# Graph message stage: a tile's two counts as one two-column product, with the right-hand columns copied into a small ring by ScalarE

## The reference, cut to what matters

```
es, ev = ys[dst], yv[dst]
m0a = wA * es * sh0
m0b = wD * einsum('eud,ed->eu', ev, sh1) * INV_SQRT3
m1a = wB[:, :, None] * es[:, :, None] * sh1[:, None, :]
m1b = wC[:, :, None] * ev * sh0[:, :, None]
ns  = segment_sum(concatenate([m0a, m0b], axis=1), src, num_segments=N)
nv  = segment_sum(concatenate([m1a, m1b], axis=1), src, num_segments=N)
deg = segment_sum(ones(n_edges), src, num_segments=N)
os_ = (ns * dn[:, None]) @ w2_s * inv2 + sc_s        # dn = rsqrt(max(deg, 1))
```

## Time and profile before

| | |
|---|---|
| time, median of 3 runs | 6061.02 us (6052.65 to 6061.88) |
| the profiled execution, its own time | 6073.1 us |
| its span, first to last instruction | 6071.4 us |
| PE busy | 5657.3 us, 93% |
| PEld busy | 4550.0 us, 75% |
| DVE busy | 5431.3 us, 89% |
| ACT busy | 3457.0 us, 57% |
| POOL busy | 4647.0 us, 77% |
| stage (c), first to last scatter start | 2655.0 to 5760.7 us |

### The profile page before, as it was taken

How to read it: one execution, slowest core, us unless ns; L and a number is a source line. 1 busy time by engine, 2 the same in 40 slices (tenths; PEclk the granted TensorE clock), 3 DMA queues, 4 the chain that set the end, 5 groups by cost and what they waited for, 6 DMA issues and landing times.

```text
span 6071.4 us, 211848 instructions
## 1 busy us (share of the span) xinstructions
PE 5657.3 (93%) x41086; PEld 4550.0 (75%) x41087; DVE 5431.3 (89%) x17528; ACT 3457.0 (57%) x12685; POOL 4647.0 (77%) x3868
## 2 busy tenths in 40 slices
PE   7899999999999997789999999999999999999876
PEld 5455555555555555579999999999999999999765
DVE  2899999999999998989999999999999999999777
ACT  2566666666666665655555555555555555555466
POOL 2777777777777774458888888888888888888877
PEclk9899999999999999999999999999999999999999
DMA  6799999999999996469999999999999999999997
GB/s 202 216 269 267 268 269 267 266 268 267 266 267 267 266 268 182 136 148 178 178 178 178 178 177 177 178 175 176 178 176 177 178 177 176 176 177 175 155 278 229
DMA packets 1269411, 1272.43 MB, mean 210 GB/s; under 512 B 220911, under 2 KB 1205744, under 8 KB 1269264
## 3 DMA queue, kind: packets, MB, share of 16 engines
q0 software_dynamic: 328176, 468.28, 46.2%
q1 hardware_dynamic: 941186, 803.62, 45.7%
HBM read 682.35 MB, written 588.89 MB: 209 GB/s over the span
## 4 chain that ended last, share of the span: by engine, by line
PE 52%; DMA 14%; issue 11%; DVE 9%; SPq 4%; DVEq 4%; ACT 3%; POOL 2%; ACTq 0%; POOLq 0%
DMA part<-arena,c_idx 13%; PE PS L905 10%; PE PS L1008 9%; PE PS L990 8%; PE PS L895 6%; PE PS L979 6%; PE PS L1023 6%; PE PS L1006 4%; SPq L437 2%; DVE big L1279 2%; DVEq L362 2%; POOL part L603 2%; DVE big L1217 1%; PE PS L846 1%; DVE big L1225 1%
## 5 line engine op out<-in xcount | busy, mean ns | idle before, releaser
L603 POOL DMA_INDIRECT part<-arena,c_idx x1664 | 2596.6, 1560 | 530.2 <-issue 341.5
L574 POOL DMA_INDIRECT big<-h_tab,big x1664 | 1631.6, 981 | 526.0 <-issue 364.4
L905 PE MATMUL PS<-big 128*128 128x260 f32 x3328 | 972.5, 411 | 155.6 <-DVE big L1217 148.6
L1008 PE MATMUL PS<-w2m,arena 128*128 128x128 f32 x6656 | 1103.7, 288 | 0.0
L905 PEld LDWEIGHTS PS<-big 128*128 128x128 f32 x3328 | 556.1, 189 | 443.4 <-issue 333.1
L1008 PEld LDWEIGHTS PS<-w2m,arena 128*128 128x128 f32 x6656 | 876.9, 192 | 0.0
L990 PE MATMUL PS<-arena 128*128 128x256 f32 x3328 | 860.7, 381 | 15.3 <-ACT arena L781 14.8
L1225 DVE TENSOR_TENSOR big<-big,PS 128x260 f32 x1664 | 700.0, 421 | 168.7 <-PE PS L905 118.5
L678 ACT ACTIVATE big<-PS,arena 128x128 f32<-128x128 f32 x1664 | 513.3, 359 | 502.7 <-PE PS L895 501.4
L780 ACT COPY arena<-PS 128x512 f32<-128x512 f32 x832 | 488.8, 588 | 545.0 <-DMA part<-arena,c_idx 493.3
L757 ACT COPY arena<-PS 128x384 f32<-128x384 f32 x1664 | 719.2, 487 | 28.4 <-PE PS L979 3.0
(11 more groups left out here) (194 smaller groups left out, 10950.0 us busy)
## 6 DMA issues: line engine op xcount, KB each, us to landing
w_tab<-big SPq DMA_DIRECT2D x416, 520.0 KB
arena<-w_tab SPq DMA_DIRECT2D x1664, 130.0 KB
part<-arena SPq DMA_DIRECT2D x1664, 32.1 KB
ot_tab<-big SPq DMA_DIRECT2D x416, 128.0 KB
arena<-ot_tab SPq DMA_DIRECT2D x416, 128.0 KB
arena<-src_tab SPq DMA_DIRECT2D x416, 128.0 KB
big<-part SPq DMA_DIRECT2D x392, 128.5 KB, 3.0
big<-h_tab,big POOLq DMA_INDIRECT x1664
```

The costliest lines, as they stand in the source:

```text
L574: pool.indirect_dma_start(hg[:, s, k, :], None, h_tab, bass.IndirectOffsetOnAxis(ap=sidx[:, s, k:k + 1], axis=0)).then_inc(s_hg[s], 16)
L603: pool.indirect_dma_start(part[q], bass.IndirectOffsetOnAxis(ap=c_idx[:, s, k:k + 1], axis=0), o_cmb[:, s, k, :], None, compute_op=ALU.add ...
L905: mm(PS[:, 2 + k % 2, 0:HW], oh[:, p, k, :], hg[:, p, k, :], start=True, stop=True).then_inc(s_agg, 1)
L1008: last = mm(o_v[:, k, 2 * j:2 * j + 2, :].rearrange("p j u -> p (j u)"), midT[:, k, 1 + j, :], w2m[:, (1 + 2 * j) * MUL:(3 + 2 * j) * MUL] ...
```

## The change

Three edits. TensorE's `count` now makes one product of two columns for each tile in place of two products of one column, so its weights are loaded once for a tile and not twice. Its right-hand side is `c_vr`, a new ring of four slots with two tiles of two bf16 columns each. The second column of all of it (`rank`) is written once by VectorE at the start of the program, in place of the copy to `rank_b`. The first (`valid`) is written by ScalarE in each step, just ahead of its copy to `c_sh`. Two waits come with it: ScalarE waits for `s_ccnt` before it overwrites a slot, and TensorE's `count` waits for `s_csh`, the semaphore of the copy to `c_sh`.

```diff
-        rank_b = sb("rank_b", [P, 1], BF16)
...
+        c_vr = sb("c_vr", [P, TURN, PAIR, 2], BF16)
...
                 if there(u):
                     wait(act, s_cw[s], landed(u, s, PAIR))
                     wait(act, s_cov, u - 3)
+                    wait(act, s_ccnt, u - 3)
+                    a.copy(c_vr[:, s, :, 0], valid[:, ds(u * PAIR, PAIR)])
                     a.copy(c_sh[:, s, :, :], wt[:, s, :, D + 1:D + 4]).then_inc(s_csh, 1)
...
                 def count():
                     wait(pe, s_cnum, u - 3)
+                    wait(pe, s_csh, u - 2)
                     for k in range(PAIR):
-                        eq = same[:, o, k, :].bitcast(BF16)[:, 1::2]
-                        mm(counts[:, k, 0:1], eq, valid[:, ds((u - 3) * PAIR + k, 1)], start=True, stop=True)
-                        last = mm(counts[:, k, 1:2], eq, rank_b[:, :], start=True, stop=True)
+                        last = mm(counts[:, k, :], same[:, o, k, :].bitcast(BF16)[:, 1::2], c_vr[:, o, k, :],
+                                  start=True, stop=True)
                     last.then_inc(s_ccnt, 1)
...
-            v.tensor_copy(rank_b[:, :], rank)
+            v.tensor_copy(c_vr[:, :, :, 1], rank_i[:, 0:1].bitcast(F32).to_broadcast([P, TURN * PAIR]).rearrange(
+                "p (s k) -> p s k", s=TURN))
```

## The result

The change makes the kernel slower: 6101.58 us (median of 4 runs, 6096.34 to 6105.8) against 6060.51, a ratio of 1.0065 (95% interval 1.0052 to 1.0078). In a later group of five rounds on one chip it was 1.0056 (1.0042 to 1.007). The forecast was 6058, in a range of 6036 to 6080.

What follows compares the result with a forecast made beforehand. GpSimd's scatter pitch, 3.695 us a step, was taken to bound stage (c). Of 5.0 us waiting for data 3 came off, the 28.3 us of longer scatters stayed: 6061.0 - 3 = 6058 us, range 6036 to 6080.

Steps and rivals of the forecast that it cites:

- GpSimd's pitch bounds the stage: Stage (c): GpSimd's scatters, 3.695 us a step, set the pace; at most 33.3 of TensorE's 41.6 us can be had.
- bare pitch: GpSimd in stage (c): 1663 start-to-start distances of 1.8475 us, unstretched and without waits, 3072.4 us.
- TensorE's pitch 3.65 us, ScalarE's copy and the waits at no cost: Stage (c): TensorE's step falls from 3.70 to 3.65 us; ScalarE's 0.2 us copy is hidden, the new waits cost nothing.
- Where TensorE's time goes: Stage (c): ScalarE's 493 us wait on landed scatters rises by about 40, TensorE's on ScalarE from 14.8 to 30-50.
- the 28.3: Stage (c): 28.3 us by which some scatters run longer than the median, left unchanged in the forecast.
- The DMA variant: DMA engines have no room, so landings get later with any gain, ending at the forecast; chance 0.61 together with it.
- The slower rival: Stage (c): VectorE's L1388 moves over scatter starts and holds them up to 0.2 us; at most 33 us more; chance 0.17.
- at the edge: Stage (c): VectorE's comparison in a quiet stretch runs 0.07 us over the next scatter's start without lengthening it.
- the sign set for this rival, 1575: Profile after: a mean scatter (L603) above 1575 ns would show that other VectorE operations came over scatter starts.
- The scatter is held until about its end: GpSimd: a two-SBUF-input VectorE operation still running some 0.1 us after a scatter's start holds the scatter until it finishes.

Runs made afterwards that it cites:

- f3: Kernel before, four count products kept, with c_src loaded ahead of wt and VectorE's comparison moved ahead in its step; ratio 0.9963 to the kernel before.
- f4: Kernel before with only the load of c_src moved ahead of the loads of wt; ratio 0.9947 to the kernel before.
- g2: The same kernel as f4, run on another chip; ratio 0.9969 to the kernel before there.
- e1: Kernel before plus ScalarE's new copy and both new waits, counts still made in four products; ratio 1.0004 to the kernel before.
- e2: Changed kernel with each two-column product made twice, so TensorE's pitch is back at 3.70 us; ratio 1.0000 to the kernel before.
- e6: Changed kernel with the load of c_src moved ahead of the two loads of wt; ratio 0.9990 to the kernel before.
- e8: Changed kernel with VectorE's 128x512 comparison cut into two of 128x256; ratio 1.0033 to the kernel before.
- g1: The same kernel as e6, run again on the chip of g2; ratio 0.9996 to the kernel before.
- f1: Changed kernel unaltered, measured again in a later group; ratio 1.0056 to the kernel before.

## Why the prediction was wrong

- *GpSimd's pitch bounds the stage*: right. The bare pitch held in every run, and the best of them stand 7 to 12 us above 3072.4. TensorE ended early as before (21.0 us idle ahead of stage (d)), and its saving bought nothing. Only in f3, f4 and g2, which keep the four products and have hardly a scatter held, is TensorE at 3.700 us the slower of the two, by 0.005 us a step.
- *TensorE's pitch 3.65 us, ScalarE's copy and the waits at no cost*: right, within 0.14% (e1, e2).
- *Where TensorE's time goes*: its wait on ScalarE rose to 61.1 us, above the 30 to 50 forecast; ScalarE's wait on landed scatters rose by 182 us, not by 40.
- *"A late landing throws VectorE back over a scatter's start just as before, since that phase is set by the landing and not by TensorE. So I leave the 28.3."* This is the step that failed. The phase is set by the landing, but the landing is set by SyncE's loads, and these follow TensorE and VectorE. They go out 0.2 us earlier against the scatter in the median, `c_src` before 1.7 us in 106 cases instead of 14, and the scatter then lands 0.5 to 1 us later. ScalarE's copy, TensorE and VectorE are thrown back, and the comparison lies over the next scatter's start. The term measured 56.6 us instead of 28.3, and with e2, e6 and e8, which each weaken one link, 26, 37 and 18 us of the scatters' time come back.
- *The DMA variant*: I wrote that later landings end "at the forecast too". They don't: GpSimd had no more to wait for (6.7 us left, against 5.0), but behind the late landings more scatters were held.
- *The slower rival* named the right place, a VectorE operation over a scatter's start, and gave at most 33 us more. The operation was wrong: L1388 made 0.9 us, and the comparison that was already at the edge made 47.7 of the 56.6. The mean of 1577 ns passed the sign set for this rival, 1575.
- *"The scatter is held until about its end"*, for an operation that runs on some 0.1 us after the start: borne out. Up to 0.12 us of overlap the comparison held none; beyond that the hold grew with the overlap, less 0.12 us.

What stays open: why a load issued 1.5 us after the scatter's start goes with a later landing than one issued at 0.1 or 2.3 us, and whether it is `c_src` or the pair of `wt` ahead of it. The trace shows when, not how the packets queue. And why stage (a) is slower on the second chip, where it moved 203 GB/s (g1, 400 to 2300 us) against 268 (f1), stays open too.

## What to carry to other kernels

Before you speed up an engine, take the pitch of each engine from start to start; where a second one has the same pitch, the saving can't come out, and the quicker engine runs up against the ring between them. Then ask what the quicker engine will issue earlier, and beside which transfer that lands: here the kernel lost 0.6% by 0.05 us a step of TensorE, and the kernel before gained 0.5% by moving one 128 KB load ahead of two others. Here a producer a little slower than its consumer (3.700 against 3.695 us) kept the ring empty and the late transfers harmless.

## What the runs showed of the hardware

- At the same traffic an indirect scatter's landing differs by about 1 us with the time at which SyncE's loads go out beside it: 6.22 us where `c_src` (128 KB, with two loads of `wt` just ahead) goes out 1.0 to 1.7 us after the start, 5.21 us at 2.0 to 3.0 (changed kernel). With the order swapped (e6) the 90th percentile fell from 6.60 to 5.89 us.
- A scatter's instruction on GpSimd is held, by up to 0.54 us (1.54 to 2.08), when VectorE's comparison with two SBUF inputs runs over its start by more than 0.12 us; the same comparison begun later under the scatter costs neither anything (0.69 us at 3968.10).
- The same kernel took 12% longer on another chip (6770 against 6067 us) with stage (c) unchanged to within 3 us (f4 3079.1, g2 3081.5).
